# Row maxima of causal attention: mask added by VectorE or by TensorE, and other warm-up matmuls

## What is computed

```python
att = jnp.einsum('bhqd,bhkd->bhqk', q, k) / HD ** 0.5
mask = jnp.tril(jnp.ones((t, t), dtype=bool))
att = jnp.where(mask[None, None], att, -jnp.inf)
att = jax.nn.softmax(att, axis=-1)
y = jnp.einsum('bhqk,bhkd->bhqd', att, v)
...
x = _layernorm(x + attention(x), axis=-1)
x = _layernorm(x + mixture_of_experts(x), axis=-1)
```

## Time and profile before

| what | us |
|---|---|
| runs: median (lowest, highest of 3) | 596.62 (594.53, 596.81) |
| span of the profiled execution, first to last instruction | 595.8 |
| median of the runs less that span | 0.8 |
| VectorE busy in the span | 439.8 |
| TensorE busy in the span | 552.3 |
| ScalarE, GpSimd busy in the span | 366.3, 268.4 |

### The profile page before, as it was taken

The page is one execution under the profiler, slowest core; times in us unless marked ns, Lnnn a source line. Parts: engine busy times, 40 slices in busy tenths (PEclk is TensorE's granted clock), DMA queues, the critical chain, the costliest instruction groups (busy, mean ns, idle before and its releaser), DMA issues.

```text
span 595.8 us, 12306 instructions
## 1 busy us (share of the span) xinstructions
PE 552.3 (93%) x3831; PEld 368.1 (62%) x3831; DVE 439.8 (74%) x1183; ACT 366.3 (61%) x831; POOL 268.4 (45%) x319
## 2 busy tenths in 40 slices
PE   8989999999999899999998888899999999999691
PEld 4636433443453255444432477799999999998481
DVE  2378989899997189989970169988788888886362
ACT  3435777867667787867678265356667666666032
POOL 5132368221185364444767530447744544454131
PEclk9989999999999699999999799999999999999696
DMA  5842490700421914101222422386544334420882
GB/s 142 153 101 27 113 260 23 141 0 15 81 86 66 174 31 74 50 2 42 70 66 92 153 73 57 102 239 202 166 138 143 106 119 126 120 87 15 317 318 70
DMA packets 53741, 64.95 MB, mean 109 GB/s; under 512 B 8123, under 2 KB 47438, under 8 KB 53680
## 3 DMA queue, kind: packets, MB, share of 16 engines
q1 hardware_dynamic: 45952, 46.45, 30.7%
q0 software_dynamic: 7104, 17.60, 8.4%
q10 hardware_dynamic: 624, 0.13, 0.1%
HBM read 32.49 MB, written 25.76 MB: 98 GB/s over the span
## 4 chain that ended last, share of the span: by engine, by line
PE 64%; DVE 10%; ACT 6%; POOL 6%; DMA 5%; issue 5%; SPq 1%; ACTq 0%; POOLq 0%; DVEq 0%
PE psH L1880 13%; PE psO L1680 7%; PE psS L1695 7%; PE psT L1665 7%; DVE MX L1364 4%; POOL xs_scratch L1005 3%; PE psS L1757 3%; PE psX L1848 3%; PE psG L1891 3%; ACT prob L1108 2%; DMA wA_raw<-in_L_ffn_w_routed_dram 2%; PE psY L1903 2%; PE psY L1907 2%; PE psY L1905 2%; PE psY L1906 2%
## 5 line engine op out<-in xcount | busy, mean ns | idle before, releaser
L1108 ACT ACTIVATE prob<-psT 128x512 f32<-128x512 f32 (+3 forms) x384 | 163.6, 497 | 65.5 <-PE psT L1665 64.5
L1364 DVE TENSOR_REDUCE MX<-psS 128x1 f32<-128x512 f32 (+3 forms) x344 | 181.9, 595 | 10.9 <-PE psS L1695 6.5
L1665 PE MATMUL psT<-QS,KS 98*128 98x512 bf16 (+3 forms) x384 | 105.8, 335 | 5.6 <-ACT prob L1108 3.3
L1072 POOL DMA_INDIRECT y_scratch<-ys,dst x80 | 77.8, 972 | 73.6 <-ACT ys L1258 59.0
L1695 PE MATMUL psS<-KS,QS 96*128 96x512 bf16 (+3 forms) x384 | 106.1, 328 | 1.0 <-DVE y L1389 0.2
L1005 POOL DMA_INDIRECT xs_scratch<-x1row,slotu x64 | 64.4, 1006 | 61.8 <-DVE slotu L1445 44.5
L1680 PE MATMUL psO<-prob,V 128*32 128x512 f32 (+3 forms) x768 | 84.7, 515 | 5.6 <-POOL prob L1034 5.5
L1880 PE MATMUL psH<-wU,xh 128*128 (+1 forms) x384 | 81.5, 334 | 0.0
L1034 POOL TENSOR_SCALAR_AFFINE_SELECT prob<-prob 128x512 f32<-128x512 f32 x64 | 40.9, 642 | 71.0 <-ACT prob L1108 70.8
L1665 PEld LDWEIGHTS psT<-QS,KS 98*128 98x128 bf16 x384 | 34.6, 99 | 59.9 <-ACT prob L1108 39.0
L1695 PEld LDWEIGHTS psS<-KS,QS 96*128 96x128 bf16 x384 | 35.6, 98 | 45.3 <-DVE MX L1364 23.4
(11 more groups left out here) (257 smaller groups left out, 998.8 us busy)
## 6 DMA issues: line engine op xcount, KB each, us to landing
xs<-xs_scratch SPq DMA_DIRECT2D x80, 134.0 KB
y<-y_scratch SPq DMA_DIRECT2D x16, 512.0 KB, 11.9
QS<-qp SPq DMA_DIRECT2D x48, 128.0 KB, 4.2
wU_raw<-in_L_ffn_w_routed_dram SPq DMA_DIRECT2D x32, 176.0 KB, 3.2
xs_scratch<-padrow SPq DMA_DIRECT2D x1, 2144.0 KB
xs_scratch<-padrow SPq DMA_DIRECT2D x16, 134.0 KB
x1row<-in_L_attn_x_dram SPq DMA_DIRECT2D x4, 512.0 KB, 6.8
out_dram<-x1row SPq DMA_DIRECT2D x8, 256.0 KB, 2.3
```

What stands on the lines that cost most here:

```text
L1072: nc.gpsimd.indirect_dma_start(y4_dram, bass.IndirectOffsetOnAxis(ap=dst[:, n % NSEL, t:t + 1], axis=0), ys[:, n % NYS, t, :], None, bound ...
L1108: nc.scalar.activation(prob[:, step % NPROB, h, 0:HALF - c0], ps[:, 0:HALF - c0], ACT.Exp).then_inc(s_Tfree, 1)
L1364: nc.vector.tensor_reduce(out=MX[:, c0 // HALF, heads[0]:heads[-1] + 1, i - TH * q], in_=src, op=ALU.max, axis=AX_X).then_inc(s_Sfree, 1)
L1665: mm(ps[:, 0:HALF - c0], KS[b][:, g, j * P:(j + 1) * P], QS[:, QAT[(k // 2) % NSLOT], g % 2 * G + h, c0:HALF], start=True, stop=True).then ...
```

## The change

One-head units that reach the diagonal get no mask matmul. VectorE reads their scores and a 512-column mask mask_w (zeros, with the old triangle as its last 128 columns, named mask_b), adds them, writes the sum back over the scores in PSUM and keeps the row maximum, in one tensor_tensor_reduce. Units of two or four heads stay as they were. span() tells the planner of it, so SEQ may come out in another order. At the start, four of the nine warm-up matmuls stay; six on 64 rows and eight on 32 rows, each of 256 columns of fp32r ones ("probe"), take the place of the others; VectorE fills probe with a memset and a copy ahead of its other work, and TensorE waits for that (s_probe).

```diff
@@ span
-        return len(heads) * (n / 2400 + (0.062 if c0 + n == (i + 1) * P else 0.009)), 0, (len(heads) * n + 65) / 960 + extra
+        onchip = 0.053 if len(heads) > 1 else 0.0
+        if len(heads) == 1 and c0 + n == (i + 1) * P:
+            extra += 0.07
+        return len(heads) * (n / 2400 + 0.009 + onchip), 0, (len(heads) * n + 65) / 960 + extra
@@ buffers
-        mask_b = sb("mask_b", [P, P], BF16)
+        place[0] = moe_end
+        mask_w = sb("mask_w", [P, HALF], BF16)
+        mask_b = mask_w[:, HALF - P:HALF]
+        place[0] = at_wA
+        probe = sb("probe", [P, 2 * P], F32R)
+        probe_raw = sb("probe_raw", [P, 2 * P])
@@ gpsimd
-            for m in (ident, ident_b, mask_b, padrow):
+            for m in (ident, ident_b, mask_w, padrow):
                 nc.gpsimd.memset(m[:, :], 0.0).then_inc(s_const, 1)
@@ vector
+            nc.vector.memset(probe_raw[:, :], 1.0).then_inc(s_probe, 1)
+            dve.wait_ge(s_probe, 1)
+            nc.vector.tensor_copy(probe[:, :], probe_raw[:, :]).then_inc(s_probe, 1)
@@ vector, smax
-                    nc.vector.tensor_reduce(out=MX[:, c0 // HALF, heads[0]:heads[-1] + 1, i - TH * q], in_=src, op=ALU.max,
-                                            axis=AX_X).then_inc(s_Sfree, 1)
+                    if len(heads) == 1 and c0 + cols == (i + 1) * P:
+                        nc.vector.tensor_tensor_reduce(
+                            ps[:, 0:cols], ps[:, 0:cols], mask_w[:, HALF - cols:HALF], scale=1.0, scalar=-3.0e38,
+                            op0=ALU.add, op1=ALU.max,
+                            accum_out=MX[:, c0 // HALF, heads[0], i - TH * q:i - TH * q + 1]).then_inc(s_Sfree, 1)
+                    else:
+                        nc.vector.tensor_reduce(out=MX[:, c0 // HALF, heads[0]:heads[-1] + 1, i - TH * q], in_=src, op=ALU.max,
+                                                axis=AX_X).then_inc(s_Sfree, 1)
@@ tensor, start
-            for n in range(WARM):
+            for n in range(WARM // 2):
                 mm(psS[:, 0, :], ones_b[:, :], ones_b[:, :].unsqueeze(1).to_broadcast([P, HALF // P, P]), start=True, stop=True)
+            pe.wait_ge(s_probe, 2)
+            for n in range(6):
+                a = n % 2 * 64
+                mm(psS[:, n % 2, 0:2 * P], probe[a:a + 64, 0:P], probe[a:a + 64, :], start=True, stop=True)
+            for n in range(8):
+                a = n % 4 * 32
+                mm(psS[:, n % 4, 0:2 * P], probe[a:a + 32, 0:P], probe[a:a + 32, :], start=True, stop=True)
@@ tensor, smax
-                    masked = c0 + cols == (i + 1) * P
+                    masked = len(heads) > 1 and c0 + cols == (i + 1) * P
```

More of the change, by code:

```diff
@@ L689, in attention_moe @@
         s_m2 = sem("s_m2")
+        s_probe = sem("s_probe")
         s_mrow = sem("s_mrow")
@@ L974, in _ @@
                                         pattern=[[-1, P]], channel_multiplier=1).then_inc(s_const, 1)
-            nc.gpsimd.affine_select(out=mask_b[:, :], in_=mask_b[:, :], compare_op=ALU.is_ge, fill=NEG, base=0,
+            nc.gpsimd.affine_select(out=mask_b, in_=mask_b, compare_op=ALU.is_ge, fill=NEG, base=0,
                                     pattern=[[-1, P]], channel_multiplier=1).then_inc(s_const, 1)
@@ L1699, in run @@
                             d = e * dist + cols - P
-                            last = mm(ps[:, d:d + P], ident_b[:, :], mask_b[:, :], start=False, stop=True)
+                            last = mm(ps[:, d:d + P], ident_b[:, :], mask_b, start=False, stop=True)
                     last.then_inc(s_S, 1)
```

## The result

The changed kernel takes 611.48 us (median of 4 runs, 609.97 to 613.04); beside it on the same chip the kernel before took 596.02 (4 runs). The ratio is 1.0267, interval 1.0239 to 1.0294: 15.5 us slower, where 591.3 was forecast and the range ended at 603. The span of the profiled execution is 611.2 us against 595.8.

What follows compares the result with a forecast made beforehand. In attention VectorE (90% busy) and TensorE were taken to hold each other, TensorE's path ending later. Span 595.8 - 5.8 (half of TensorE's saving) + 0.5 (start) = 590.5, with 0.8 for the median 591.3 us; range 583 to 603.

Steps and rivals of the forecast that it cites:

- Part 1: TensorE in attention: 192 one-head diagonal mask matmuls go, 0.06 us each, 11.5 us less.
- Part 2: VectorE in attention: the new instruction costs 0.065 us more in 192 units, 12.5 us; bounds 0 and 48 us.
- the end at 0: Lower bound of VectorE's extra cost per new instruction: 0, if the second output comes with the main one.
- How the two meet: Attention's end: TensorE's path (323.5 us) is later than VectorE's (317), whose extra work fills idle time; -5.8 us counted.
- less lucky order: A worse order of the items, counted within the slower outcomes; no size given, chance 0.04.
- Dear output: VectorE in full attention stretches: second output at 0.20 us per unit costs +11 us, 607.5 us; chance 0.18.
- Half rate: VectorE's new instruction streams at half the rate, another 72.5 us, about 660 us in all; chance 0.03.
- The scatters: Attention's end hangs on GpSimd's scatters, so TensorE's saving becomes waiting: 597 us, or 594 with part saved; chance 0.20.
- Both idle stretches close: VectorE's idle stretches in attention, near 200 us and after 300, close: -15 to -18 us, 580 us; chance 0.10.
- the hole near 200 us: VectorE almost idle at 184 to 209 us of attention; its extra work was to go there, making it shorter.
- A cold start: Kernel start: TensorE's lower clock lasts into the first projections and nothing is won, 599 us; chance 0.03.
- The start: Before the first weight products: wider mask memset and new warm-up matmuls, together taken as +0.5 us.

Runs made afterwards that it cites:

- Experiment 2: The kernel before with only the new planner prices, so old instructions in the changed kernel's order: 1.0238 of the kernel before.
- experiments 6: The changed kernel with the 2.1 MB fill issued with the sixth query load instead of the fourth: 1.0063 of the kernel before.
- 9: The changed kernel in the old order up to the fifth group's maxima, in the new order from there: 1.0062 of the kernel before.
- experiment 1: The changed kernel with the old planner prices, which give back the old order: 0.9941 of the kernel before.
- experiment 3: The kernel before with the new warm-up matmuls alone: 1.0022 of the kernel before.
- Experiments 4: The changed kernel with weight loads and splits put behind the second-pass items they followed in the old order: 1.0485 of the kernel before.
- 8: The changed kernel, its planner admitting wB's low parts with VectorE's booked clock up to 1.5 us ahead instead of 0.3: 1.0324 of the kernel before.
- experiment 5: The changed kernel in the old order with the old nine warm-up matmuls: 0.993 of the kernel before, 623.6 us against 628.7.
- 15: The changed kernel in the old order, experiment 1 once more on another chip: 0.99 of the kernel before.

## Why the prediction was wrong

**Part 1, TensorE's saving: right in kind and count.** 64 mask matmuls are left. In the old order the new instructions gave 0.9941, 0.993 and 0.99, that is 3.7, 4.4 and 6.3 us of about 630. "I count half of TensorE's saving as reaching the end: -5.8 us" fits them, though the half came from no row, and so its size is partly luck; the forecast's own ratio, 591.3 / 596.6 = 0.991, lies inside all three intervals.

**Part 2, VectorE's price: too high.** 0.065 us per unit was taken; 0.008 is measured in front of a reduction and some 0.05 in a run of new instructions, 3.2 us in all in place of 12.5. The rows of similar pairs priced the second instruction as if it held the engine each time; in most places it overlaps with the next one altogether. This error was on the safe side. That the Trainium skill (VectorE: DVE Perf Modes, "Two Vector instructions with no wait between them") counts such an op as two instructions agrees with the two rows; but the prediction's "by it the end at 0 would drop out" made too much of the count, for the price is near that end.

**How the two meet: this step failed.** "Nothing else moves", the sum says. That holds for the old order, where VectorE's 12.5 us had a hole to go into and the DMAs stood where the earlier trace rows show them. It was applied to a kernel whose planner gets new durations and writes every engine's list anew. The prediction had the fact in hand ("the planner, not the data, places them") and said of Part 2 "no queue entry of SP is added or removed": true, and they were reordered. A "less lucky order" had 0.04. Experiment 2 shows that the order by itself, with the old instructions, makes a loss of 2.4%, no smaller than the whole loss on those chips; in the result's trace it is 13.5 us by the end of attention.

**The part of the loss that is located.** About half, by experiments 6 and 9 on their chips, is one inversion in SP's queue: a latency-critical DMA (one that the next matmuls wait for) behind 2.1 MB of padding. On the result's chip the third group's end moves by 11.0 us.

**The rivals.** *Dear output* had the right sign and would have given 607.5, near the time, by a mechanism that is refuted: the price is 0.008 to 0.05, 3.2 us in all. That the time came near is chance. Nor do waits for banks measure such a price, as the prediction would have it ("much longer than 23 us"): the waits of L1720 are 16.7 + 11.2 = 27.9 us in the changed kernel against 23.3; in the old order (experiment 1) they are 38.6 against 25.0 in experiment 3 on the same chip, and its attention ends 12.1 us sooner in the two traces (the times differ by 10.4 us in these two executions, and by 5.4 in the medians). A kernel can wait more for banks and be faster. *Half rate* is refuted too: 512 columns follow in 0.606 us. *The scatters* are not in the chain of the last 33 us of the changed kernel's attention. *Both idle stretches close* came true for the hole near 200 us, and did not help, for it was closed by a first pass that ran later. *A cold start* came in part: the transposes began at 5.85 us, but they and seven products ran at the slower step until 8.89 us, 2.4 us longer than before, and the first projection began 0.7 us late. It is no cause of the loss: the first group ends at 63.0 us in both.

**The start.** +0.5 was predicted. Experiment 3 has 1.0022 with an interval of 0.4% to either side, 2.6 us, so it agrees with +0.5 and with nothing.

**What stays open.** The lag of the fifth group (30.4 us in the changed kernel for the step that took 25.8; 30.8 with the early stall away, in experiments 6 and 9) and the last group's 7.7 us have no single cause that I could show. The last group's trace has the weight splits on ScalarE, the idle TensorE and 12 us of the lower clock behind it, but no run takes the splits away without moving them into other groups. Argued only: plan() booked VectorE 0.07 us more for each diagonal unit, so it placed 15 units fewer in the first four groups, where they would have fit beside other work, and made room for them later; and it booked the weights last. Experiments 4 and 8 moved the weights alone to two other places, and both were worse.

**A version that beats both.** The VectorE mask in the old order, with the old warm-up (experiment 5) or the new (1 and 15): 0.993, 0.9941 and 0.99 of the kernel before. On one chip, experiment 5 took 623.6 us and the changed kernel 637.3.

## What to carry to other kernels

Where a planner writes the order from a table of durations, an entry in that table is part of the change, and a larger one than the instruction it describes: hold the list fixed while the instruction is measured, put the measured price in, and then see whether the new list is better than the old one. Where a changed list makes a kernel slower, compare the ends of the stages in both traces and look for the first step; it here showed a small, urgent DMA behind a large idle one in one queue. An argument over total busy time by engine cannot see either.

## What the runs showed of the hardware

- An add that writes its full result back to PSUM, with the row maximum as second output, takes 8 ns more from start to start than a plain reduction of as many columns where a reduction follows it; its read of the accumulator (0.14 us in its row) runs wholly beside that. In a run of such instructions most take some 50 ns more (0.648 against 0.598 us at 512 columns).
- A DMA on SP's queue that was issued 0.64 us behind a fill of 2.1 MB took 10.36 us from issue to landing, and 2.70 us elsewhere in that trace; the end of the group that waited came 6.7 us sooner when the fill was moved.
- Behind a stretch of 5.5 us without TensorE work the granted clock was 0.51 in the next 7 us; behind the idle TensorE at 318.6 us it was 0.50 for 12 us, and eight matmuls took 1.94 us instead of 1.06.
- Six fp32r matmuls on 64 rows took 1.01 us and eight on 32 rows 0.80 at 256 columns each: with their start and end overlapping they took 1.67 us, where five of 512 columns on 128 rows took 5 x 0.43 = 2.15.
- On the other chips the kernel before takes 5 to 7% longer (629 to 635 us), and the traces there have waits of up to 9.45 us that the profile can't name. Up to the seventh group's end (175.7 us in the kernel before, 175.5 in experiment 3) the times are the same.
